# GNN layers on one core: ScalarE's high features behind a pair's first high part, unit transposes part by part, and two low parts behind the last diagonal

## What is computed

```python
# x: 4096 x 256, adj: 4096 x 4096 of 0 and 1
Wh = x @ W.T
sim = Wh @ Wh.T / (|Wh_i| |Wh_j| + 1e-8)
alpha = softmax(where(adj > 0 or i == j, sim, -inf), axis=1)
x1 = layernorm(x + alpha @ Wh)
agg = (adj > 0) @ x1 / max(deg, 1)
out = relu(concat(x1 @ W_self + b_self, agg @ W_nb + b_nb) @ W_comb + b_comb)
result = layernorm(x1 + out)
```

## Time and profile before

| | |
|---|---|
| runs (3) | 839.12, 839.24, 840.9 us |
| profiled execution | 840.58 us, span 838.8 us |
| PE busy | 821.3 us (98%) |
| DVE busy | 590.7 us (70%) |
| ACT busy | 343.0 us (41%) |
| share of the DMA queue of SP | 71.6% |
| granted TensorE clock over the span | 0.999 |

### The profile page before, as it was taken

The page is one execution under the profiler, slowest core; times in us unless marked ns, Lnnn a source line. Parts: engine busy times, 40 slices in busy tenths (PEclk is TensorE's granted clock), DMA queues, the critical chain, the costliest instruction groups (busy, mean ns, idle before and its releaser), DMA issues.

```text
span 838.8 us, 17690 instructions
## 1 busy us (share of the span) xinstructions
PE 821.3 (98%) x6591; PEld 655.0 (78%) x6591; DVE 590.7 (70%) x1472; ACT 343.0 (41%) x553; POOL 73.6 (9%) x177
## 2 busy tenths in 40 slices
PE   8999999999999999999999999999999999999997
PEld 7866667777777777777777777678888888888886
DVE  3788898888878888888898989998254333343333
ACT  4866655565554655565556555554100000000000
POOL 3400000001000000001001002012011110111011
PEclk9999999999999999999999999999999999999999
DMA  8969998989999799979999989996103330330300
GB/s 212 254 159 228 257 236 218 272 219 263 215 232 270 189 277 211 238 234 253 251 257 218 240 237 233 236 222 232 27 20 127 120 114 20 120 121 13 120 20 20
DMA packets 223485, 155.26 MB, mean 185 GB/s; under 512 B 159921, under 2 KB 186818, under 8 KB 222370
## 3 DMA queue, kind: packets, MB, share of 16 engines
q1 hardware_dynamic: 223202, 153.68, 71.6%
q0 software_dynamic: 192, 0.41, 0.3%
HBM read 95.83 MB, written 20.99 MB: 139 GB/s over the span
## 4 chain that ended last, share of the span: by engine, by line
issue 78%; POOL 6%; DVE 1%; POOLq 1%; PE 0%; ACT 0%; DVEq 0%; ACTq 0%
POOL rstd L590 4%; POOL var_eps L588 2%; POOLq L589 0%; POOLq L587 0%; PE ps L1291 0%; PE ps L1293 0%; PE ps L1292 0%; DVE mgroup L1045 0%; DVE prob_lo L1027 0%; POOLq L592 0%; DVE mix_extremes L866 0%; DVE prob_hi L1026 0%; ACT mask L689 0%; ACT mgroup L705 0%; DVE work L1021 0%
## 5 line engine op out<-in xcount | busy, mean ns | idle before, releaser
L1291 PE MATMUL ps<-feat,prob_hi 128*128 128x257 f16 x1024 | 280.3, 274 | 6.3 <-DVE big L1010 2.6
L1293 PE MATMUL ps<-feat,prob_lo 128*128 128x257 f16 x1024 | 279.2, 273 | 0.0
L1292 PE MATMUL ps<-feat,prob_hi 128*128 128x256 f16 x1024 | 278.1, 272 | 0.0
L1420 PE MATMUL ps<-big,mgroup 128*128 128x257 f16 x992 | 219.2, 273 | 0.0
L1421 PE MATMUL ps<-big,mgroup 128*128 128x256 f16 x992 | 219.2, 273 | 0.0
L689 ACT ACTIVATE mask<-work 128x1024 fp8e4<-128x1024 f16 x112 | 114.9, 1048 | 100.2 <-DVE work L1021 100.2
L1291 PEld LDWEIGHTS ps<-feat,prob_hi 128*128 128x128 f16 x1024 | 99.6, 97 | 35.8 <-issue 6.7
L1292 PEld LDWEIGHTS ps<-feat,prob_hi 128*128 128x128 f16 x1024 | 100.5, 98 | 24.6
L649 ACT ACTIVATE work<-ps 128x512 f32<-128x512 f32 (+2 forms) x144 | 79.9, 556 | 94.9 <-PE ps L1244 91.9
L1293 PEld LDWEIGHTS ps<-feat,prob_lo 128*128 128x128 f16 x1024 | 99.3, 97 | 13.7
L1420 PEld LDWEIGHTS ps<-big,mgroup 128*128 128x128 fp8e4 x992 | 97.1, 98 | 12.1
(11 more groups left out here) (126 smaller groups left out, 795.4 us busy)
## 6 DMA issues: line engine op xcount, KB each, us to landing
adj_sb<-adjT SPq DMA_DIRECT2D x128, 512.0 KB, 5.0
mask_spill<-mask SPq DMA_DIRECT2D x128, 128.0 KB, 4.9
mgroup<-mask_spill SPq DMA_DIRECT2D x8, 2048.0 KB, 7.9
xres<-x SPq DMA_DIRECT2D x8, 512.0 KB, 5.3
out<-rows SPq DMA_DIRECT2D x32, 128.0 KB, 1.7
feat<-xT SPq DMA_DIRECT2D x7, 512.0 KB, 6.2
mgroup<-mgroup SPq DMA_TRANSPOSE x112, 3.9
norm_bc<-norm_row_dram SPq DMA_DIRECT2D x7, 256.0 KB, 6.5
```

Of the source, the lines that this page charges most:

```text
L1291: pe.matmul(acc(D + 1), prob_hi[:, s, cols], feat_hi_of(g)[:, r, 0:D + 1], start=start, stop=False)
L1292: pe.matmul(acc(D), prob_hi[:, s, cols], feat_lo_of(g)[:, r, :], start=False, stop=False)
L1293: return pe.matmul(acc(D + 1), prob_lo[:, s, cols], feat_hi_of(g)[:, r, 0:D + 1], start=False, stop=stop)
L1420: pe.matmul(agg_ps(q, D + 1), lhsT, z_hi_of(g)[:, r, 0:D + 1], start=(jb == 0), stop=False)
```

## The change

Four things change. (1) In row 0 ACT makes the high features of group b inside pair (0, b), behind exponential and high part of its first tile, instead of at the end of pair (0, b-1); `unit_heads(7)` moves from behind pair (0, 1) to behind pair (0, 2). (2) SP no longer turns a unit at one go behind a pair: the high half of unit 6 goes behind the store of m = 1 in pair (0, 3) and its low half behind the store of m = 3; unit 7 likewise in pair (0, 4). (3) The last two pieces of row 5's normalisation (low parts of x1, q = 2 and 3) go behind `diagonal(7)`; SP turns x1 of row 5 behind row 7's residual load; a wait for `rows_ready` stands ahead of `attention_out`. (4) The other 12 pieces of pair (6, 7) are spread anew over its nine places.

```diff
-            def turn_units(g):
+            def turn_units(g, halves=range(2)):
                 sync.wait_ge(unit_hi_ready, g + 1)
                 sync.wait_ge(unit_ready, g + 1)
-                for half, to in enumerate((unitT_hi, unitT_lo)):
+                for half in halves:
+                    to = (unitT_hi, unitT_lo)[half]
...
                     if b == G - 1 and m == 1:
                         load_residual(a)
+                    if a == 0 and b in (3, 4) and m % 2:
+                        turn_units(PROMPT + b - 3, [m // 2])
...
-                    if a == 0 and b in (2, 3):
-                        turn_units(PROMPT + b - 2)
                 if a == G - 1:
                     load_residual(a)
                 if a == G - 2:
                     turn_x1(G - 4)
-                    turn_x1(G - 3)
...
+            turn_x1(G - 3)
             masks_stored(2)
...
                     high(r)
+                    if a == 0 and b > 1 and r == 0:
+                        act.wait_ge(feat_ready, 1)
+                        if b >= GB:
+                            act.wait_ge(feat_free, 1 if b < PROMPT else 2)
+                        split_high(b)
...
-            def next_features(b):
-
-                if b == 1:
-                    unit_heads(G - 1)
-                if b == 3:
-                    act.wait_ge(feat_free, 1)
-                if b == PROMPT - 1:
-                    act.wait_ge(feat_free, 2)
-                if b + 1 < G:
-                    split_high(b + 1)
...
                     pair_far(a, b)
-                    if a == 0:
-                        next_features(b)
+                    if a == 0 and b == 2:
+                        unit_heads(G - 1)
...
             def attention_out(a, t):
 
                 dve.wait_ge(attn_done, t + 1)
+                wait(dve, rows_ready, a * GB)
...
-            between = []
+            between, carried = [], []
             for a in range(G):
                 diagonal(a, between)
+                for piece in carried:
+                    piece()
+                carried = []
...
+                    if a == G - 2:
+                        carried, between = between[-CARRIED:], between[:-CARRIED]
                     pair_far(a, b, between)
```

More of the change, by code:

```diff
@@ L52 @@
 ACT_X1 = G - 3
+CARRIED = 2
 EPS_MATTERS_BELOW = 0.5
@@ L689, in unit_kept, with split_high @@
                 act.activation(mask[:, u % 4, :], kept(m), ACT.Copy, saturate=False).then_inc(mask_ready, 1)
+            def split_high(g):
+                act.activation(feat_hi_of(g)[:, :, 0:D], wh_of(g), ACT.Copy, scale=scales[:, 0:1]).then_inc(act_feat_hi, 1)
             def pair_far(a, b):
@@ L720, in pair_far @@
                     x1_head(a - 1, 3)
-            def next_features(b):
-                if b == 1:
-                    unit_heads(G - 1)
-                if b == 3:
-                    act.wait_ge(feat_free, 1)
-                if b == PROMPT - 1:
-                    act.wait_ge(feat_free, 2)
-                if b + 1 < G:
-                    split_high(b + 1)
-            def split_high(g):
-                act.activation(feat_hi_of(g)[:, :, 0:D], wh_of(g), ACT.Copy, scale=scales[:, 0:1]).then_inc(act_feat_hi, 1)
             for a in range(G):
```

## The result

| | before | after |
|---|---|---|
| median of 6 runs each | 839.58 us (839.05 to 840.9) | 845.01 us (844.4 to 846.2) |
| ratio | | 1.0064, interval 1.0051 to 1.0077 |
| profiled execution, span | 840.58, 838.8 us | 844.78, 843.0 us |
| PE, DVE, ACT busy | 821.3, 590.7, 343.0 us | 823.3, 590.2, 344.0 us |
| granted clock over the span | 0.999 | 0.994 |

The change makes the kernel slower by 5.4 us (0.64%). The forecast was slower, by 3.5 us, 842.7; the measured time lies in the range, near its upper end. The two profiled executions differ by 4.2 us.

What follows compares the result with a forecast made beforehand. PE, busy 98% of the span, was taken as the bound. From the median, -0.92 - 0.15 - 2.7 + 5.95 + 1.85 - 0.5 = +3.5 us gave 842.7 us; own range 840.9 to 845.5, 8-in-10 range 838.0 to 845.5.

Steps and rivals of the forecast that it cites:

- The wait, +5.95: End of pair (0, 4): DVE waits 6.1 us for unit 7's late low half, delaying PE by 5.95 us.
- The clock, +1.85: After PE's stall of about 6 us the clock falls to half pace, costing 1.85 us (0 to 3.7).
- The rival in which the clock holds: The stall comes but PE's clock stays up or recovers at once: +1.7 us, 840.9; chance 0.20.
- The first pair change, -0.92: Earlier high part lets DVE start sooner; PE's 0.77 us wait at 72.93 goes whole: -0.92 us.
- Pair (0, 3), -2.7: Unit 6 no longer ahead of the pair's transposes; three PE stalls go: -2.7 us, other end -2.0.
- my first three terms: The gains of -0.92 (first pair change), -0.15 (a later pair change) and -2.7 us (pair (0, 3)).
- the 6 us that I called the most to be won: PE's listed idle times from 50 us to row 7's end, with 0.15 us each: about 6 us, 0.7%.
- Row 6, -0.5: Respread pieces and later low parts shorten PE's waits, some returning near `values(3)`: -0.5 us, between -0.8 and +0.3.
- SP's queue blocks: Each added transpose holds SP 3.28 us; low half 1.4 us later, pair (0, 3) keeps some stalls: 845 us; chance 0.07.

Runs made afterwards that it cites:

- away_later: The changed kernel with DVE's second `units_away` moved from behind pair (0, 4) to a piece inside pair (0, 5): 838.18 us.
- pair_earlier: The changed kernel with unit 6 turned in pair (0, 2) and unit 7 in pair (0, 3), high half waiting for its high part alone: 837.43 us.
- both_at_m1: The changed kernel with both halves of a unit turned behind the second store of pairs (0, 3) and (0, 4): 839.86 us.
- kept_warm: The changed kernel with 24 dummy matmuls on PE during its stall in pair (0, 4), DVE's wait untouched: 842.5 us.
- turns_only: The kernel before plus only SP's moved unit transposes (unit 6 by halves in pair (0, 3), unit 7 in pair (0, 4)): 845.62 us.
- act_only: The kernel before plus only ScalarE's part (high features behind the first high part, unit heads of group 7 behind pair (0, 2)): 837.98 us.
- carried_only: The kernel before plus only row 5's last two low parts behind the last diagonal and the other pieces respread: 839.49 us.
- whole_turns: The changed kernel with SP's unit transposes back as before, a whole unit behind pairs (0, 2) and (0, 3): 837.81 us.

## Why the prediction came out as it did

*That it is slower, and where*: right. The memset behind pair (0, 4) waits 6.60 us for `unitT_lo`, PE stands 6.77 us ahead of the copy that follows, and the clock falls. Moving the wait away (away_later), or the transposes (pair_earlier), takes 6.8 to 8.3 us off.

*The wait, +5.95*: measured +6.47, 6.77 of stall less the 0.30 that stood there before. The wait was 6.60 against 6.1, as DVE arrived 0.45 us earlier than I had taken: at 116.16, where 120.6 on the old clock is 116.6 on the new one (3.99 less). Two terms inside it missed and cancelled. The low half was issued at 117.46 and not at 115.9 (119.9 less 3.99), since the second transposes and the high half held SP longer (3.67 and 2.74 us). It landed 5.2 us later, not 6.8. For the landing, were no better a neighbour than the earlier trace rows; it lies about midway. both_at_m1 shows that it grows with the loads ahead: 3.8 us where those two loads go in behind it.

By the Trainium skill (DMA: Bandwidth & Descriptors, section "Queues, rings and completion order") a ring's descriptors are served in order. The runs agree with it: 5.2 us with two loads ahead of the transpose, 3.8 us with them behind it.

*The clock, +1.85*: right, 1.99 by the copies of block results and 2.0 by kept_warm (in turns_only it was 1.46, see the last section). The rival in which the clock holds, with its +1.7 us, falls.

*The first pair change, -0.92*: right; act_only gives -1.1 us by the medians (-2.5 to -0.4 by the interval), and the 0.77 us are gone. The unit heads behind pair (0, 2) cost nothing, as forecast: behind them ACT's high part ends at 81.35, 0.2 us before DVE's low part begins at 81.53. From ACT's timeline after:

```profile
78.52 1.69 ACT L617 ACTIVATE feat<-big,unit_mul 128x256 f16<-128x256 f32 x4
...
80.72 0.63 ACT L711 ACTIVATE mgroup<-work 128x512 f16<-128x512 f32 x1
```

*Pair (0, 3), -2.7*: this is the step that was mis-sized. In the one trace that I had, it was nearly right: up to pair (0, 4) the gain was 3.99 us, or 3.71 without the 0.28 from ahead of row 0's first pair, against the 3.77 of my first three terms. But the sum was put on the median, and the median doesn't hold all of these stalls. In act_only and carried_only the same pair loses 1.23 us in one stall, not 2.26 in three, and in whole_turns nothing. So at most about 1.4 us of the 2.7, with its 0.15, can be counted on the median; at least 1.3 was a chance of the profiled execution, which at 840.58 stood 1.3 us above the median that I started from. I named that difference and let it pass. With -1.4 in its place the sum is +4.8, and with the 0.52 and 0.14 us that wait and clock were larger, +5.5, against 5.4 measured. That this fits so closely is partly luck, since the -1.4 is not firm. turns_only points to about -1.0: from block 0 of pair (0, 4) to block 0 of (0, 5) its copies take 23.75 us (114.73 to 138.48) and before's 16.20, so wait and slow clock cost 7.55, but its median is only 6.5 above before's. And away_later (838.18), with the transposes in their new place and no wait at the memset, is not under whole_turns (837.81), which has them in the old one. How much a typical execution gains in pair (0, 3), between nothing and 1.4 us, stays open.

My list of PE's stalls was not complete either. It left out the 1.00 us at 531.53, as row 6 begins, and 0.28 us at 139.56, so the losses in that trace were above the 6 us that I called the most to be won.

*Row 6, -0.5*: PE's wait there fell from 1.36 to 0.97 us (forecast: by 0.33), the 0.28 us at 558.68 went, and 0.19 us came back at `values` (forecast 0.25). In the trace each step is there. The median of carried_only is +0.4 us from before, with an interval of -0.6 to +1.1, which just takes in -0.5. It is too small to be seen.

*SP's queue blocks*, the rival at 845: its time came out, its mechanism by half. The low half did go out late, by 1.6 us (117.46 against 115.9) where the rival had 1.4. But no stall is left in pair (0, 3), and the high half issued in 1.40 and 2.74 us, not 3.28 each.

## What to carry to other kernels

When a transfer is moved later, look for the wait that it feeds, on every engine: splitting the unit transposes did free the queue in pair (0, 3), but their deadline, a memset that nobody moved, was 6.6 us too early for them; the same split one pair earlier, with ScalarE's part, wins 0.2 to 0.3% over the kernel before, most of which ScalarE's part may give alone (0.18%). A stall of the matmul engine of some microseconds should be priced with the slow clock behind it, here 1.5 to 2 us on top of 6 to 6.5. And stalls that end with a DMA are to be read in more than one execution before they are counted as a gain: a profile above its median holds losses that the median doesn't.

## What the runs showed that I had not expected

- A stall of 3.25 us brings the clock down, too, and the fall shows only after PE is back at work: granted 1.00 from 121 to 123, where PE returns at 122.34, then 0.51 while PE is busy throughout. Half the stall cost 1.67 us of clock, nearly as much as the 6.77 us one (1.99). The rows show why. In the changed kernel the clock is already low when PE comes back at 125.87, and the shares 0.54 (123 to 125) and 0.75 (129 to 131) put the low spell at 123.2 to 130.0: PE works 4.1 us of it. In both_at_m1 the spell is 123.0 to 126.4 (by 0.51 and 0.64), and PE works all 3.4 us of it. In turns_only PE comes back later, at 127.61, and the share of 0.59 in the row below ends the spell at 130.6: 3.0 us. Half of these times is 2.1, 1.7 and 1.5 us; what PE lost against the 9.41 us of before is 1.99, 1.67 and 1.46.

```profile
129.00:131.00 2.00, 2.00 (x13) 1.45 (x12) 1.40 (x4) 1.95 (x3) 0.00 (x0) 0.59 1.23 172
```

- Stalls of 1.96 us in away_later and 1.98 us in whole_turns left the clock at 1.00; whole_turns from PE's return at 122.17 on:

```profile
122.00:124.00 2.00, 1.83 (x17) 1.66 (x18) 2.00 (x6) 0.67 (x1) 0.00 (x0) 1.00 0.86 115
124.00:126.00 2.00, 2.00 (x20) 1.78 (x19) 1.39 (x4) 1.50 (x3) 0.00 (x0) 1.00 1.22 177
```

- The same transpose at the same place held SP's queue for 2.74 us in the changed kernel and 1.41 us in kept_warm, where nothing ahead of it in the queue's order differs (kept_warm's row):

```profile
112.53 1.41 SPq L421 DMA_TRANSPOSE unitT_hi<-feat  x1
```

- One program's executions spread over 2 to 4 us (835.3 to 839.1 for pair_earlier). Two profiled ones differ by a late transpose (1.5 us) and by 0.5 us that lay ahead of it.
